# The first projections of three feed-forward stages as seven block products instead of eight

## Time and profile before

| what | value |
| --- | --- |
| median of 3 runs | 2758.71 us (2757.53 to 2760.18) |
| span of the profiled execution | 2765.5 us |
| TensorE matmuls busy | 2553.8 us (92%) |
| VectorE busy | 1544.1 us (56%) |
| ScalarE busy | 1062.2 us (38%) |
| GpSimd busy | 439.6 us (16%) |
| the chain that ended last: share on TensorE | 81% |

### The profile page before, as it was taken

How to read it: one execution, slowest core, us unless ns; L and a number is a source line. 1 busy time by engine, 2 the same in 40 slices (tenths; PEclk the granted TensorE clock), 3 DMA queues, 4 the chain that set the end, 5 groups by cost and what they waited for, 6 DMA issues and landing times.

```text
span 2765.5 us, 61215 instructions
## 1 busy us (share of the span) xinstructions
PE 2553.8 (92%) x24673; PEld 1796.7 (65%) x24673; DVE 1544.1 (56%) x3588; ACT 1062.2 (38%) x2136; POOL 439.6 (16%) x432
## 2 busy tenths in 40 slices
PE   6997899999999849997999999997998899699999
PEld 5886466666666536675888888884443677456555
DVE  5888678878788573112555555443333599722221
ACT  5885456555565402211323333322111677310110
POOL 2322001011010013422011111010000455300000
PEclk9999899999999959998999999998999999899999
DMA  5000000000000143534000000000000233100000
GB/s 210 3 2 2 20 27 26 23 30 23 23 30 23 42 113 93 142 90 137 1 0 0 0 0 0 0 1 0 0 0 0 77 108 113 51 8 16 8 15 16
DMA packets 72126, 101.97 MB, mean 37 GB/s; under 512 B 10865, under 2 KB 50289, under 8 KB 71473
## 3 DMA queue, kind: packets, MB, share of 16 engines
q1 hardware_dynamic: 65840, 91.46, 10.3%
q0 software_dynamic: 6144, 8.56, 1.6%
HBM read 67.20 MB, written 32.80 MB: 36 GB/s over the span
## 4 chain that ended last, share of the span: by engine, by line
PE 81%; DMA 7%; DVE 6%; issue 2%; ACT 2%; POOL 1%; SPq 1%; DVEq 0%; ACTq 0%; POOLq 0%
PE psW L322 16%; PE psW L315 9%; PE psS L1377 8%; DMA rotated<-work 6%; PE psP L437 4%; PE psP L1343 4%; PE psP L430 4%; PE psP L1337 4%; PE psS L1371 4%; PE psO L1337 4%; PE psO L1343 4%; PE psS L381 3%; PE psO L414 3%; PE psW L529 3%; PE psO L346 2%; PE psP L397 2%
## 5 line engine op out<-in xcount | busy, mean ns | idle before, releaser
L322 PE MATMUL psW<-r,work 128*128 128x512 f32 x1024 | 483.4, 606 | 1.0 <-DVE work L773 1.0
L1270 POOL TENSOR_TENSOR work<-work 128x512 f32<-128x512 f32 x128 | 132.0, 1042 | 1147.1 <-DVE work L807 1147.1
L322 PEld LDWEIGHTS psW<-r,work 128*128 128x128 f32 x1024 | 181.3, 192 | 163.6 <-issue 157.9
L315 PE MATMUL psW<-work,r 128*128 128x128 f32 x2048 | 244.2, 278 | 1.0 <-DVE work L773 1.0
L315 PEld LDWEIGHTS psW<-work,r 128*128 128x128 f32 x2048 | 235.6, 193 | 3.5 <-DVE work L773 1.4
L1377 PE MATMUL psS<-r,work 128*128 128x256 f32 x960 | 211.2, 381 | 5.7 <-DVE work L1450 5.3
L1377 PEld LDWEIGHTS psS<-r,work 128*128 128x128 f32 x960 | 181.2, 190 | 33.2 <-DVE work L1450 6.1
L1184 ACT ACTIVATE work<-work 128x512 f32<-128x512 f32 x128 | 80.1, 626 | 277.2 <-DVE work L786 277.2
L1534 ACT ACTIVATE work<-psP 128x512 f32<-128x512 f32 x64 | 38.2, 597 | 285.9 <-PE psO L1337 285.9
L529 PE MATMUL psW<-work,r 128*128 128x128 f32 x1024 | 135.0, 286 | 7.3 <-ACT work L1084 6.5
L1450 DVE TENSOR_TENSOR work<-work,psO 128x512 f32<-128x512 f32 x64 | 44.0, 688 | 168.0 <-ACT work L1534 168.0
(11 more groups left out here) (284 smaller groups left out, 4652.3 us busy)
## 6 DMA issues: line engine op xcount, KB each, us to landing
r<-in_l_fc SPq DMA_DIRECT2D x16, 1024.0 KB
rotated<-work SPq DMA_DIRECT2D x60, 256.0 KB
work<-mod_rows SPq DMA_DIRECT2D x64, 128.0 KB, 2.8
work<-rotated SPq DMA_DIRECT2D x30, 256.0 KB
r<-in_l_w SPq DMA_DIRECT2D x2, 3072.0 KB, 14.4
x<-in_x SPq DMA_DIRECT2D x8, 512.0 KB, 9.7
gather_table<-work SPq DMA_DIRECT2D x32, 128.0 KB, 1.8
moe_sum<-work SPq DMA_DIRECT2D x32, 128.0 KB, 1.7
```

The lines of the kernel that those rows point to most:

```text
L315: ins = nc.tensor.matmul(ps[:, q * P:(q + 1) * P], w[:, k, lo + q * P:lo + (q + 1) * P], L.hT[:, k, :], start=(k == 0), stop=(k == KC - 1))
L322: ins = nc.tensor.matmul(ps[:, 0:width], L.hT[:, k, :], w[:, k, lo:lo + width], start=(k == 0), stop=(k == KC - 1))
L1270: nc.gpsimd.tensor_tensor(E, E, halves(L.rs)[i].unsqueeze(2).broadcast_to([P, 8, N]), ALU.mult).then_inc(L.s[f"prob{i}"].sem, 1)
```

## The change

The product of a weight matrix with two feature halves (rows) and the activations with two feature halves and two token halves (columns of 256) is a 2 by 2 by 2 block product, eight block products. The change uses Strassen's scheme in a form with seven products and reused sums. The weight blocks are `a11, a12, a21, a22`: the two feature halves by the two halves of the hidden width ("moe", "l2"), or by gate and up ("l3"). The activation blocks `b11, b12, b21, b22` are 128 features by 256 tokens each.

- GpSimd makes four sums of weight blocks (`pool_weight_sums`), one of them in place of `a21`: for every expert, and once for "l2" and for "l3".
- VectorE makes four sums of activation blocks behind `modulate` (`t1` to `t4`, kept in `Q.mix`).
- TensorE makes the seven products A to G for each chunk `m` of 256 rows (`M` is 2, in "l3" 4). A product is two matmuls of 256 columns. B, D, E and G accumulate in one bank (`BANK_A[m % 2]`), C and F in another (`BANK_D[m % 2]`), A has `psW1` (`BANK_C`).
- After B, after D and after E the running sum is copied out of the bank before the next product adds to it: `p1` by VectorE in "moe" and "l2" and by ScalarE in "l3", `u2` and `u3` by ScalarE. VectorE adds A, C and F to these copies (`c11`, `c22`, `c12`). The fourth quarter of the output is left in the bank by G.
- ScalarE then applies the activation, in "moe" and "l2" in pieces of 256 tokens.
- The loops over groups are written out.
- In group 0 of the expert stage VectorE's `hot` work moves behind modulate(1), and norm(1) behind the last sum; TensorE's slot sums move behind result(0). GpSimd makes an expert's weight sums ahead of the gather for the expert after it.

The core of the diff:

```diff
+                if kind == "l3":
+                    self.products = "B0 A0 D0 C0 E0 B1 G0 D1 F0 C1 E1 A1 G1 B2 F1 D2 C2 E2 A2 G2 B3 F2 D3 C3 E3 A3 G3 F3".split()
+                    self.sums = [f"{n}{m}" for m in range(4) for n in ("c22_", "c11_", "left_", "c12_", "right_")]
+                    self.parts = ["p1_0", "u2_0", "u3_0", "gate_0"]
+                    self.parts += [f"{n}{m}" for m in range(1, 4) for n in ("p1_", "u2_", "up_", "u3_", "gate_")] + ["up_4"]
+                else:
+                    self.products = "B0 A0 D0 C0 E0 B1 G0 D1 F0 C1 E1 A1 G1 F1".split()
+                    self.sums = "p1_0 c11_0 c22_0 p1_1 c12_0 c22_1 c11_1 c12_1".split()
+                    self.parts = "u2_0 u3_0 h11_0 u2_1 h22_0 h21_0 u3_1 h12_0 h22_1 h11_1 h21_1 h12_1".split()
+                self.s |= signals("f_product", NG * len(self.products))
+                self.s |= signals("f_summed", NG * len(self.sums))
...
+        def pool_weight_sums(g, Q, n, u):
+
+            a11, a12, a21, a22 = Q.blocks[u]
+            s2, s3, s4 = Q.extra[u]
+            done = Q.s["f_sum"]
+            nc.gpsimd.tensor_tensor(s3, a11, a21, ALU.subtract).then_inc(done.sem, 1)
+            after(g, done, 4 * n + 1)
+            nc.gpsimd.tensor_tensor(a21, a21, a22, ALU.add).then_inc(done.sem, 1)
+            after(g, done, 4 * n + 2)
+            nc.gpsimd.tensor_tensor(s2, a21, a11, ALU.subtract).then_inc(done.sem, 1)
+            after(g, done, 4 * n + 3)
+            nc.gpsimd.tensor_tensor(s4, a12, s2, ALU.subtract).then_inc(done.sem, 1)
...
+            def product(bank, w, m, h, first=True):
+
+                for i in range(2):
+                    at = (2 * m + i) * P
+                    ins = nc.tensor.matmul(bank[:, 256 * i:256 * i + 256], w[:, at:at + P], h,
+                                           start=first and i == 0, stop=i == 1, skip_group_check=True)
+                return ins
...
+                def A(m):
+                    after(pe, *Q.summed(t, "c11", m - 1))
+                    product(BANK_C, a12, m, b21).then_inc(done, 1)
+
+                def B(m):
+                    after(pe, *(Q.summed(t, "left", m - 2) if Q.kind == "l3" else Q.part(t, "h21", m - 2)))
+                    product(BANK_A[m % 2], a11, m, b11).then_inc(done, 1)
+
+                def C(m):
+                    after(pe, *Q.summed(t, "c12", m - 2))
+                    product(BANK_D[m % 2], s1, m, t1).then_inc(done, 1)
+
+                def D_(m):
+                    after(pe, *(Q.part if Q.kind == "l3" else Q.summed)(t, "p1", m))
+                    product(BANK_A[m % 2], s2, m, t2, False).then_inc(done, 1)
+
+                def E(m):
+                    after(pe, *Q.part(t, "u2", m))
+                    product(BANK_A[m % 2], s3, m, t3, False).then_inc(done, 1)
+
+                def F_(m):
+                    after(pe, *Q.summed(t, "c22", m))
+                    product(BANK_D[m % 2], s4, m, b22, False).then_inc(done, 1)
+
+                def G(m):
+                    after(pe, *Q.part(t, "u3", m))
+                    product(BANK_A[m % 2], a22, m, t4, False).then_inc(done, 1)
...
-                    if Q.kind == "l3":
-                        after(pe, Q.s["f_he"], t * FJ + (j - 1))
...
+                B(1)
+                G(0)
+                D_(1)
+                F_(0)
+                if Q.kind == "l2" and t > 0:
+                    back(t - 1)
+                C(1)
+                E(1)
+                A(1)
+                G(1)
+                for m in range(2, M):
+                    B(m)
+                    F_(m - 1)
+                    D_(m)
+                    C(m)
+                    E(m)
+                    A(m)
+                    G(m)
+                early = ahead and not (Q.kind == "moe" and t == 0)
+                if early:
+                    turn(t + 1, 0)
+                F_(M - 1)
+                if early:
...
 
+            def chunks(t, rights):
+
+                for m in range(M):
+                    for right in rights:
+                        if Q.kind == "l3":
+                            after(pe, *Q.summed(t, "right" if right else "left", m))
+                        else:
...
+
             def result(t, u):
-                after(pe, Q.s["f_he"], t * FJ + FJ)
...
+            def step(t, u, ahead):
+                late_slots = Q.kind == "moe" and t == 0
                 if late_slots:
                     pe.wait_ge(rt["slots"], 2)
-                hidden(t, u, half)
+                hidden(t, u, ahead)
+                if late_slots:
+                    after(pe, *Q.summed(0, "c11", M - 1))
+                    turn(1, 0)
+                    turn(1, 1)
+                result(t, u)
                 if late_slots:
                     for i in range(2, len(GROUPS)):
                         pe_slot_sums(pe, i)
-                if ahead:
-                    turn(t + 1)
-                if late_slots:
                     for i in range(2, len(GROUPS)):
                         pe_slot_turn(pe, i)
                     pe.wait_ge(rt["slots"], len(GROUPS))
...
+                t1, t2, t3, t4 = Q.mix
+                b11, b12 = Q.gT[:, 0, 0:256], Q.gT[:, 0, 256:512]
+                b21, b22 = Q.gT[:, 1, 0:256], Q.gT[:, 1, 256:512]
+                nc.vector.tensor_tensor(t3, b22, b12, ALU.subtract)
+                ch.link(nc.vector.tensor_tensor(t1, b12, b11, ALU.subtract))
+                ch.link(nc.vector.tensor_tensor(t2, b22, t1, ALU.subtract))
+                nc.vector.tensor_tensor(t4, b21, t2, ALU.subtract).then_inc(Q.s["f_h"].sem, 1)
+
...
+            def first_part(t, m):
+
+                after(v, *Q.product(t, "B", m))
+                if m == 0:
+                    after(v, Q.s["f_y"], t)
+                nc.vector.tensor_copy(places(t, m)[0], two(BANK_A[m % 2])).then_inc(Q.s["f_summed"].sem, 1)
+
+            def c22(t, m):
+                out = places(t, m)[2]
+                after(v, *Q.part(t, "u3", m))
+                after(v, *Q.product(t, "C", m))
+                nc.vector.tensor_tensor(out, two(BANK_D[m % 2]), out, ALU.add).then_inc(Q.s["f_summed"].sem, 1)
+
+            def c11(t, m):
+                out = places(t, m)[0]
+                after(v, *Q.product(t, "A", m))
+                after(v, *(Q.part if Q.kind == "l3" else Q.summed)(t, "p1", m))
+                nc.vector.tensor_tensor(out, two(BANK_C), out, ALU.add).then_inc(Q.s["f_summed"].sem, 1)
+
...
+            def left_product(t, m):
+
+                after(v, *Q.product(t, "G", m))
+                after(v, *Q.part(t, "gate", m))
+                if m == 0:
+                    after(v, Q.s["f_y"], t)
+                nc.vector.tensor_tensor(Q.hid[:, 2 * m:2 * m + 2, 0:256], two(BANK_A[m % 2]), places(t, m)[0], ALU.mult
+                                        ).then_inc(Q.s["f_summed"].sem, 1)
...
+            def hidden_l3(t, ahead):
+                if ahead:
+                    norm(t + 1, (t + 1) % 2)
+                for m in range(M):
+                    c22(t, m)
+                    c11(t, m)
+                    left_product(t, m)
+                    c12(t, m)
+                    right_product(t, m)
+
...
+            def hidden_two(t, ahead):
+
+                first_part(t, 0)
+                late = Q.kind == "moe" and t == 0
+                c11(t, 0)
+                if ahead and not late:
+                    norm(t + 1, (t + 1) % 2)
+                c22(t, 0)
+                first_part(t, 1)
+                c12(t, 0)
+                if Q.kind == "l2" and t > 0:
+                    add(t - 1)
+                c22(t, 1)
+                c11(t, 1)
+                c12(t, 1)
+                if Q.kind == "l2" and t > 0:
+                    measure(t - 1)
+                if late:
+                    norm(1, 1)
...
+            def step(t, u, ahead):
                 ch.reset()
...
-                ch.reset()
-                if Q.kind == "moe" and is_first(t):
+                if Q.kind == "l3":
+                    hidden_l3(t, ahead)
+                else:
+                    hidden_two(t, ahead)
+                if ahead:
+                    modulate(t + 1)
+                if Q.kind == "moe" and t == 0:
                     for i in range(2, len(GROUPS)):
                         dve_hot_a(i)
                         dve_hot_b(i)
-                if ahead:
-                    norm(t + 1, 1 - u, half + u)
...
+            def step(t, u):
+                if Q.kind == "l3":
+                    for m in range(M):
+                        first_part(t, m)
+                        second_part(t, m)
+                        if m > 0:
+                            gate(t, m - 1, 1)
+                        third_part(t, m)
+                        gate(t, m, 0)
+                    gate(t, M - 1, 1)
...
+                second_part(t, 0)
+                third_part(t, 0)
+                hid(t, u, 0, 0)
+                second_part(t, 1)
```

(47 more changed lines are left out.)

222 lines of the change are left out of this document (130 added, 92 removed).

## The result

The new kernel takes 2789.4 us (2786.2 to 2793.8, 4 runs) against 2758.5 of the kernel before (4 runs). The ratio is 1.0114, with a 95% interval of 1.010 to 1.0129. The direction was forecast; the time lies 21 us over the forecast and 7 over the range.

The account below looks back on a forecast made before the run. TensorE was taken to bound the feed-forward groups. Expert stage +12.3, L2 +6.5 and L3 -13.6 us gave +5.2 at full clock; +4.3 for the clock made +9.5, from 2758.7 to 2768 us, range 2746 to 2782.

Parts of the forecast that it names:

- The product, 0.874 us: Feed-forward groups on TensorE: each product takes four records, 0.874 us; saves 48 us over the three stages.
- 0.02 us of slack: Later copies in a group: 0.20 + 0.60 + 0.05 us against one product of 0.874, so barely on time.
- some 5 us more: Bound over all groups: a ScalarE copy at 0.66 instead of 0.60 us uses up the slack three times a chunk.
- The waits before D0 and D1: TensorE waits for copies: D0 1.65 us (expert), 2.17 (L2); D1 0.43 (expert, L2), 1.64 (L3).
- The start of each stage, 1.7 us: Before each stage's first product, four uncovered VectorE subtractions of 0.425 us each add 1.7 us.
- The opening of the expert stage: GpSimd's numbering and weight sums start hidden(1) 6.2 us later; gather(2) and norm(2) lengthen group 1 by 2.7 us.
- forecast as -15.3: L3 from its first product to its last result: 15.3 us shorter, 1.97 per steady group.
- Its result wait: L3, before a result: TensorE's wait of some 1.40 us for the last gate and multiplication goes.
- two falls in L2: Granted clock falls to half twice in seven L2 groups after the 2.17 us waits, 1.3 us each, 2.6 in all.
- the second ("D0 did not wait for VectorE's finish"): Expert stage and L2 group heads: wait not on TensorE's path, 25 us go, 2743 us; chance 0.16.
- The third (the clock falls at most waits): L2 and L3: clock falls to half at most waits, up to 2785 us; chance 0.12.

Follow-up runs that it names:

- the new order of L3: All four edits together, with L3's 28 products reordered so two other products stand between a copy's product and its reader: 2724.8 us, ratio 0.9878.
- The run with one-input instructions: New kernel with L3's four GpSimd weight sums replaced by same-size multiplications by one with one SBUF input: 2783.0 us, ratio 1.0082.
- the second pair: Second profiled executions of the new kernel and the kernel before, both unchanged: spans 2783.5 and 2757.6 us.

## Where the prediction was right, and where it failed

- **The product, 0.874 us: right in most, too small in some.** A, B, C and F follow each other at 0.865 us, but D, E and G, which wait for a copy, take 0.955 (E0 from 2078.55 to 2079.50, for instance). I had left 0.02 us of slack for the copy against the matmul. The weight load comes ahead of the matmul and has the same wait: 0.2 us late each time. It shows as no idle time of TensorE, only as a first matmul of 470 ns instead of 379. The bound of "some 5 us more" was priced for another reason, a slower copy, and came near by luck; the periods were 0.10, 0.19 and 0.40 us too long, 8 x 0.69 = 5.5 us, had nothing covered them. That the wait of the weight load is the cause was shown by the new order of L3.
- **The waits before D0 and D1: right.** Before D0 they are right to 0.06 us (1.60 and 2.11). D1 starts 5.01 us after D0 in the expert stage and 4.96 in L2, where 4.80 was forecast. In L3 D1 starts 1.5 to 1.6 us late (1.64). Removing the wait before D0, and L3's before D1, gave its price back; the small D1 wait of the two other stages was not removed alone.
- **The start of each stage, 1.7 us: right for the subtractions** (TensorE waits 4.67 before L2's first product, 2.96 before), and **incomplete as a step**: I looked only at what is new between modulate and the first product. I did not cost the L3 sums at all, nor name the work beside them, though they stood in the diff with their trigger. The step that failed is "**Start of each stage.** Before the first product stand four subtractions": 7.6 us were missing in it, the largest single miss. The prediction weighed contention between GpSimd and VectorE for the expert stage's opening only. The Trainium skill (SBUF — State Buffer, SBUF: two separate sides) states a rule that fits the rows: VectorE and GpSimd share a pair of ports under an exclusive lock, which a GpSimd instruction keeps for its whole length, and against which VectorE instructions with two SBUF inputs or in a two-port mode wait. The four rows that end 0.04 us after GpSimd's agree, though two of them are TENSOR_SCALARs with one SBUF input, and no row shows in which mode they ran. The run with one-input instructions does not: there, eleven of twelve went on beside GpSimd.
- **The opening of the expert stage: the right mechanism, sized too small.** Group 0 took 6.0 us longer (5.2 forecast). Group 1 took 6.6 in the second pair and 8.9 in the first (4.4 forecast with the clock): the landing after the issue and the norm were taken from quiet rows, but in this stretch the weights of the next expert and the weight sums run beside them. That these are the reason is argued from what stands side by side, not tested. The window over the stretch gives the DMA share as 1.02, that is, all DMA engines busy, and the clock as 0.76:

```profile
1074.00:1090.00 16.00, 9.16 (x52) 6.99 (x52) 3.87 (x7) 2.26 (x5) 13.56 (x12) 0.76 1.02 320
```

- **L3: right, in part by luck.** -14.8 us, forecast as -15.3. Its result wait went as expected, but the nearness of the sum comes from two misses of opposite sign: 3 us of late weight loads, and a first group that gained 2.9 us where 0.7 was forecast.
- **The clock: two falls in L2, as forecast, but the number was luck.** Two was a choice between none and all, not worked out. Of six profiles with that wait four show two slow groups each. In the two others the wait ahead of L2 was shorter: with L3's sums later there is none, and with one-input instructions one, in the last group (the clock at half for 3.4 us from 2126.2 on, and 1.6 us more). What decides stays open. The Trainium skill (TensorE: Matmul & The Clock Gate, HAM oscillation) warns of longer pauses only, and by it this term would be nothing; the falls came in groups whose only pauses were of 2.1 us and less.
- **The median against the profile.** Second profiles differ by 25.9 us, the medians by 30. The new kernel's profiled executions were the shortest of their four runs both times (granted clock 0.959 and 0.960, against 0.955 to 0.959 in the others). That would leave some 4 us lost to the clock in executions that no profile shows. But against the median of the 13 other executions of the kernel before on that chip, 2762.4, the medians differ by 26.7 us only, so these 4 us may as well be scatter; the runs do not decide it.

The rivals: the second ("D0 did not wait for VectorE's finish") was wrong for the change as it was; it put the wait's worth at 25 us, and the edit that takes the wait away gave 30, 3 of them by the clock's two falls. The third (the clock falls at most waits) had the number nearest to the result, 2785, but for another reason: it fell at two of them.

Of the 21 us missed, by the rows of the table: 6.6 ahead of L2 (the 7.6, less 1.0 at a better clock), 3.7 in the expert stage (3.0 of them in the opening), 2.0 in L2, mostly late weight loads, and 0.5 in L3, whose late loads were hidden by a first group that took 42.8 us instead of 45.7. Then 3.7 ahead of the expert stage and of L3, stretches that differ by up to 5 us between two profiles of one kernel, and about 4 between the profiles and the medians, which is as much as two medians of the kernel before differ by (3.4).

## What to carry to other kernels

When a scheme saves an eighth of the products but needs copies between them, what it brings is decided by where the copies stand. Here the same seven products were 1.1% slower than the plain eight as first written, and 1.0% faster once the two copies that TensorE had waited for longest had an engine with time for them and GpSimd's sums were moved. A second independent product between a copy's source and its reader took another 0.83 us out of every group of L3. When a change puts work on an engine that was idle, look at who else runs when its trigger fires, and not only at who waits for it: four GpSimd instructions whose results were needed only some 550 us later cost 7.6 us. And when two profiles are compared, take a second one of each first; the first pair showed 18.8 us, the second 25.9, where the medians differ by 27 to 31.

## What was not expected of the hardware

- A GpSimd instruction with two SBUF inputs of 128x1024 held single VectorE instructions of 32 elements until it ended: 1.57 to 2.38 us in place of 0.18 to 0.20. Beside one-input instructions, under way for 11.4 us, eleven of twelve such VectorE instructions took at most 0.28 us; one took 1.04 us, and the norm 1.26 us more.
- A matmul whose weight load waited 0.23 us for a copy left TensorE no idle time but took 470 ns instead of 379 ns.
- An idle time of 2.1 us at the head of a group of L2, every 30.5 us, went with a fall of the granted clock to half in two of eight groups in four profiles, in one group in a fifth, and in none in a sixth.
